# A post-norm layer of attention and a routed mixture of experts: last norm from accumulators, half-tile row buffers, two more ring slots, eleven more casts, other cast positions

## What is computed

```python
h = relu(einsum('td,ndf->ntf', flat, shared_w1) + b1)   # 2 shared experts, d_ff 1408
out = flat + einsum('ntf,nfd->td', h, shared_w2) + b2
scores = sigmoid(flat @ centroids.T) + bias              # 16 routed experts
gating = top-4 of scores, divided by their sum
out += sum_e relu(flat @ w1[e] + b1[e]) @ w2[e] * gating[e]
_layernorm(x) = (x - mean) / sqrt(var + 1e-5)
```

## Time and profile before

| what | value |
| --- | --- |
| time, median of 3 runs | 2623.97 us (2621.29 to 2628.06) |
| time of the profiled execution | 2625.21 us |
| its span, core 7 | 2623.6 us |
| spans of the other cores | 2576.4 to 2617.9 us |
| TensorE busy | 2201.3 us, 84% |
| VectorE, ScalarE, GpSimd busy | 855.9, 560.6, 378.0 us |

### The profile page before, as it was taken

How to read it: one execution, slowest core, us unless ns; L and a number is a source line. 1 busy time by engine, 2 the same in 40 slices (tenths; PEclk the granted TensorE clock), 3 DMA queues, 4 the chain that set the end, 5 groups by cost and what they waited for, 6 DMA issues and landing times.

```text
span 2623.6 us, 36177 instructions; the slowest of 8 cores (2576.4 to 2623.6 us)
## 1 busy us (share of the span) xinstructions
PE 2201.3 (84%) x13371; PEld 1205.6 (46%) x13371; DVE 855.9 (33%) x1390; ACT 560.6 (21%) x833; POOL 378.0 (14%) x583
## 2 busy tenths in 40 slices
PE   5879999989899669978977888899889897798576
PEld 3536646556465334433544545444545344344221
DVE  0234444444344334473311111113111131543454
ACT  0023433333343432301011111111111001011024
POOL 1001111010110000100021212122212202111100
PEclk9989999999999779999989988999999989898887
DMA  9599999999999799997489999989999979989963
GB/s 161 67 121 120 121 119 118 121 122 121 121 122 107 153 132 168 150 135 131 154 168 249 212 235 224 242 200 223 243 241 216 177 188 202 242 272 200 218 198 126
DMA packets 114970, 448.68 MB, mean 171 GB/s; under 512 B 16178, under 2 KB 16690, under 8 KB 105040
## 3 DMA queue, kind: packets, MB, share of 16 engines
q0 software_dynamic: 80208, 300.15, 74.8%
q1 hardware_dynamic: 34560, 145.70, 16.5%
HBM read 653.61 MB, written 145.23 MB: 304 GB/s over the span
## 4 chain that ended last, share of the span: by engine, by line
DMA 46%; PE 40%; DVE 5%; issue 4%; ACT 3%; POOL 1%; DVEq 0%; POOLq 0%; ACTq 0%; SPq 0%
DMA wpre<-w2x 11%; DMA wpre<-w1x 10%; PE PP L1210 9%; DMA ar<-w2x 8%; PE PP L1174 7%; DMA ar<-w1x 6%; DMA ar<-y_scr 5%; PE PP L815 4%; PE PP L639 3%; PE PP L793 3%; PE PP L341 3%; PE PP L360 2%; PE PP L1090 2%; ACT ar L496 1%; DMA ar<-xT 1%
## 5 line engine op out<-in xcount | busy, mean ns | idle before, releaser
L1174 PE MATMUL PP<-ar 128*128 128x256 bf16 (+1 forms) x2816 | 385.9, 296 | 81.2 <-DMA ar<-w1x 64.6
L1210 PE MATMUL PP<-ar 128*128 128x512 bf16 x1408 | 375.2, 405 | 21.0 <-DMA ar<-w2x 20.1
L1174 PEld LDWEIGHTS PP<-ar 128*128 128x128 bf16 x2816 | 279.8, 101 | 196.3 <-issue 110.3
L815 PE MATMUL PP<-ar 128*128 128x512 bf16 x704 | 214.5, 422 | 88.6 <-DVE ar L830 62.6
L341 PE MATMUL PP<-ar 128*128 128x512 bf16 x1024 | 245.8, 384 | 27.9 <-DMA ar<-wqkv 27.8
L496 ACT COPY ar<-PP 128x1024 bf16<-128x1024 bf16 (+1 forms) x192 | 153.4, 799 | 475.4 <-PE PP L485 475.4
L830 DVE SCALAR_TENSOR_TENSOR ar<-PP,ar 128x512 f32<-128x512 f32 x256 | 170.5, 688 | 229.3 <-PE PP L815 222.4
L360 PE MATMUL PP<-ar 128*128 128x256 bf16 x2048 | 241.5, 273 | 0.0
L1210 PEld LDWEIGHTS PP<-ar 128*128 128x128 bf16 x1408 | 132.3, 102 | 223.6 <-issue 106.6
L455 DVE TENSOR_REDUCE st_sb<-PP 128x1 f32<-128x256 f32 (+7 forms) x128 | 173.8, 1358 | 171.3 <-PE PP L449 162.3
L1099 DVE COPY ar<-PP 128x960 bf16<-128x960 bf16 x96 | 55.8, 599 | 503.8 <-PE PP L1090 503.7
(11 more groups left out here) (129 smaller groups left out, 1819.8 us busy)
## 6 DMA issues: line engine op xcount, KB each, us to landing
ar<-wpre SPq DMA_DIRECT2D x173, 512.0 KB, 8.2
ar<-w1x POOLq DMA_DIRECT2D x117, 512.0 KB, 15.3
ar<-w2x POOLq DMA_DIRECT2D x106, 512.0 KB, 20.5
wpre<-w2x POOLq DMA_DIRECT2D x92, 512.0 KB, 24.1
wpre<-w1x POOLq DMA_DIRECT2D x81, 512.0 KB, 24.7
ar<-y_scr SPq DMA_DIRECT2D x32, 1024.0 KB, 8.7
ar<-wqkv POOLq DMA_DIRECT2D x24, 1024.0 KB, 24.6
ar<-xT POOLq DMA_DIRECT2D x8, 1024.0 KB, 37.0
```

What stands on the lines that cost most here:

```text
L815: m = sb.mm((lambda e, j=j, w=w, bank=bank, ti=ti, dn=dn, last=last: e.matmul(psum_bank(bank), Hs[j][:, ti * 128:(ti + 1) * 128], w[:, dn ...
L1174: m = sb.either("tensor", j, *[[(lambda e, dc=dc, w=w, bank=bank, cols=cols: e.matmul(psum_bank(bank)[:, 0:cols], w[:, dc * 128:(dc + 1) * ...
L1210: m = sb.mm((lambda e, fc=fc, w=w, po=po, t=t, dn=dn, end=end: e.matmul(psum_bank(2 * t + dn), Hr(fc)[:, t * 128:(t + 1) * 128], w[:, po * ...
```

## The change

1. `precast` is issued at other places: no casts between the three weight loads of group 1, nine after them; 29 instead of 20 after the first feed-forward loads; and the rest (11) right behind `gather(0)`.
2. The list has 184 units: w1 of expert 12 is added ahead of its w2. `load_unit` now looks into `pre_mark`.
3. Two more slots (in the area of the former `y_in`) join the ring behind `gather(0)` and leave it at expert 12's start, where they become the first two of the half-tile buffers of the combine.
4. The combine loads half tiles (512 KB); a load is issued at every second step when a buffer is free, otherwise the oldest pending half is added and its buffer loaded anew. Ten half-tile buffers serve rank 3.
5. In the last group eight PSUM banks go round instead of three, L830 writes row sums by `accum_out`, squares are summed by ScalarE alone, and the scaling and the store of a tile follow one tile later. Ten half-tile adds are placed near the end of the first 128 matmuls; the other six follow one pair before each of the first three tile closings.

```diff
+PRE_FIRST = 9
+PRE_G0 = 29
-    units += [("w2", 2 + PRE_HALF, u) for u in range(FCH)]
+    units += [(kind, 2 + PRE_LAST, u) for kind in ("w1", "w2") for u in range(FCH)]
-                precast(PRE_ATTN)
+                precast(PRE_ATTN if g > 1 else 0)
         for kind in "qkv":
             next_w(kind, 1)
+        precast(PRE_FIRST)
...
+        def tail_squares(ti, parts):
+            ssq = tail_cols(ti)[1]
+            w = D // parts
+            for n in range(parts):
+                for dn in range(n * 4 // parts, (n + 1) * 4 // parts):
+                    sb.wait("scalar", *x_mark[ti, dn])
+                sb.wait("scalar", "ac")
+                sq_mark[ti] = sb.act(lambda e, n=n: e.activation(
+                    final_scr[:, n * w:(n + 1) * w], x_tm[ti][:, n * w:(n + 1) * w], AF.Square,
+                    accum_out=ssq[:, n:n + 1]))
+        def tail_scale(ti, parts):
+            s4, ssq, s1, var, rinv, bcol = tail_cols(ti)
+            sb.vchain(lambda e: e.reduce_sum(s1, s4, axis=AX.X))
+            sb.vchain(lambda e: e.scalar_tensor_tensor(var, s1, -1.0 / (D * D), s1, ALU.mult, ALU.mult))
+            sb.wait("vector", *sq_mark[ti])
+            for n in range(parts):
+                sb.vchain(lambda e, n=n: e.scalar_tensor_tensor(
+                    var, ssq[:, n:n + 1], 1.0 / D, var, ALU.mult, ALU.add))
+            sb.vchain(lambda e: e.tensor_scalar(var, var, EPS, None, ALU.add))
+            m = sb.vchain(lambda e: e.reciprocal(var, var))
+            sb.wait("scalar", *m)
+            m = sb.act(lambda e: e.activation(rinv, var, AF.Sqrt))
+            sb.wait("vector", *m)
+            return sb.vec(lambda e: e.scalar_tensor_tensor(bcol, s1, -1.0 / D, rinv, ALU.mult, ALU.mult))
...
-        precast(len(PRE_UNITS))
+        precast(PRE_G0)
         state["gen"] = dense_group(GROUPS[0], nt_outer=True)
...
         gather(0)
+        precast(len(PRE_UNITS))
+        ring["free"] += [(NSLOT, list_pe), (NSLOT + 1, list_pe)]
+        pump()
...
+        def combine_tick():
+            if not combine_load() and pend and todo:
+                combine_add()
+                combine_load()
...
+            if j == 12:
+                ring["leave"] = [NSLOT, NSLOT + 1]
+                ring["spare"] += [f for f in ring["free"] if f[0] >= NSLOT]
+                ring["free"] = [f for f in ring["free"] if f[0] < NSLOT]
+            if j >= 13:
+                todo.extend((j - 13, ti, hf) for ti in range(8) for hf in range(2))
...
-                if 13 <= j < 16:
-                    combine_step(j - 13, step)
+                if j >= 13 and step >= 2 and step % 2 == 0:
+                    combine_tick()
...
+            before = late.pop() if late else None
+            if before is not None:
+                ready = tail_scale(before, 1)
+            tail_squares(ti, 1 if ti < 7 else 2)
+            if before is not None:
+                tail_store(before, ready, False)
+            late.append(ti)
+            if ti == 7:
+                tail_store(7, tail_scale(late.pop(), 2), True)
...
+        for b in range(5):
+            give_bank(b, l2_free[b][0])
+        def close_tile(ti):
+            for _ in range(2):
+                if pend:
+                    combine_add()
+                    combine_load()
+            final_norm(ti)
+        for _ in dense_group(GROUPS[-1], bias2=True, after_tile=close_tile):
             count += 1
+            if count == 16:
+                while combine_load():
+                    pass
+            if count == 126:
+                for _ in range(10):
+                    combine_add()
+                    combine_load()
```

More of the change, by code:

```diff
@@ L48 @@
 PRE_EXPERTS = (0, 2, 4, 6, 8, 10, 14)
-PRE_HALF = 12
+PRE_LAST = 12
 def pre_units():
@@ new lines, in tail_store @@
+        def tail_store(ti, ready, last):
+            s4, ssq, s1, var, rinv, bcol = tail_cols(ti)
+            for hf in range(2):
+                xs = x_tm[ti][:, hf * 1024:(hf + 1) * 1024]
+                if last and hf == 1:
+                    sb.wait("vector", *ready)
+                    m = sb.vec(lambda e, xs=xs: e.tensor_scalar(xs, xs, rinv, bcol, ALU.mult, ALU.add))
+                else:
+                    sb.wait("scalar", *ready)
+                    m = sb.act(lambda e, xs=xs: e.activation(xs, xs, AF.Identity, bias=bcol, scale=rinv))
+                sb.wait("sync", *m)
+                sb.dma("sync", (lambda e, xs=xs, hf=hf: e.dma_start(
+                    out=out[ti * 128:(ti + 1) * 128, hf * 1024:(hf + 1) * 1024], in_=xs)), pool="store")
@@ L705, in emit @@
                 gate_scores(order[n - 1])
-        ring = {"free": [], "plan": [], "at": {}, "load": {}, "used": [], "spare": None}
+        ring = {"free": [], "plan": [], "at": {}, "load": {}, "used": [], "spare": None, "leave": []}
         for i in range(NSLOT):
@@ L744, in use @@
             if plans is None:
-                return ring_sb[0]
+                return slot_sb(0)
             sb.wait("tensor", *ring["load"][unit])
-            return ring_sb[ring["at"][unit]]
+            return slot_sb(ring["at"][unit])
         def release(unit, mark):
@@ L751, in release @@
                 return
-            ring["free"].append((ring["at"].pop(unit), mark))
+            slot = ring["at"].pop(unit)
+            ring["spare" if slot in ring["leave"] else "free"].append((slot, mark))
             pump()
@@ L778, in dense_group @@
         def dense_group(fcs, gate=None, bias2=False, after_tile=None, nt_outer=False):
+            ends = after_tile is not None
             h_ready = {}
@@ L1115, in emit @@
         y_freed = [[], []]
-        ybufs = [[y_in, None, None]]
         ring["spare"] = []
+        ybufs = []
         y_done = {}
-        def have_ybuf():
-            spare = dict(ring["spare"])
-            for s in sorted(spare):
-                if s in spare and s + 1 in spare:
-                    ybufs.append([carve(2048 * s, 4096, F32), spare.pop(s), spare.pop(s + 1)])
-            ring["spare"] = list(spare.items())
-            return len(ybufs) > 0
-        def combine_load(k, ti):
-            buf, m0, m1 = ybufs.pop(0)
-            for m in (m0, m1):
-                if m is not None:
-                    sb.wait("sync", *m)
+        pend = []
@@ L1133, in combine_load @@
+        todo = []
+        def combine_load():
+            ybufs.extend(ring["spare"])
+            ring["spare"] = []
+            if not (todo and ybufs):
+                return False
+            k, ti, hf = todo.pop(0)
+            slot, mark = ybufs.pop(0)
+            buf = slot_sb(slot).bitcast(F32)
+            sb.wait("sync", *mark)
             for i in range(13 + k):
                 sb.wait_all("sync", y_done[i])
-            for m in u_stored[-2:]:
-                sb.wait("sync", *m)
```

93 lines of the change are left out of this document (30 added, 63 removed).

## The result

| | before | after |
| --- | --- | --- |
| median of 5 runs | 2623.97 us | 2592.74 us |
| ratio, 95% interval | | 0.9857 (0.9828 to 0.9885) |
| profiled execution | 2625.21 us | 2580.38 us |
| its spans, mean of the 8 cores | 2601.8 us | 2566.6 us |

What follows compares the result with a forecast made beforehand. TensorE was taken as held back by casting DMAs in attention, DMA engines in the routed experts, VectorE in the combine and last group. From 2625.2 us, -32 + 22 - 12 - 22 - 23 = -67 gave median 2557 us, range 2514 to 2600.

Steps and rivals of the forecast that it cites:

- Early weight loads: Attention: group 1's weight loads no longer stand behind casts, so TensorE's later waits for them go; -32 us.
- 29 casts ahead of gather(0): Before expert 0: nine more casts delay gather(0), which lands 18 us later, plus 3 for the clock; +21 us.
- Eleven casts behind gather(0): Expert 0: gather(1) queues behind these casts and lands some 20 us later; +11 us (0 to +25).
- What follows from both: Gathers through later experts: +13 by the chain of waits, +34 at most by the DMA engines; taken as +22 us.
- Expert 12: Expert 12: w1 from `wpre` saves 21 us of DMA and TensorE's 10.5 us wait; -12 us (0 to -21).
- Half-tile combine: Combine, experts 13 to 15: VectorE hardly waits for loads, limited by 16 us of idle DMA time; -22 us.
- rival B: DMA engines bound the combine too, so its change and expert 12's bring nothing; 2591 us, chance 0.20 together with E.
- Last group: Last group: rank-3 adds end earlier, eight banks, norm a tile behind; 28 us less, 5 taken off for clock; -23 us.
- A: Experts and combine: the deeper ring pays in every pair and only VectorE's waits held the combine; 2518 us, chance 0.17.
- C: Last group stays bound by TensorE's lower clock, so the tail gains only 10 us; 2570 us, chance 0.09.
- D: From gather(0) on, late casts stay wholly on the path, 94 us, and DMA-bound gains are lost; 2663 us, chance 0.08.
- E: Attention: early loads do nothing because another wait takes their place; 2589 us alone, counted within rival B's 0.20.

Runs made afterwards that it cites:

- e1_early: Kernel before, with only attention's new cast positions (none between group 1's three loads, 29 instead of 20 casts ahead of gather(0)): 2631.48 us, ratio 0.9913.
- e6_drop9: Changed kernel with w1 and nine w2 units of expert 12 loaded directly, 20 casts ahead of gather(0), none behind: 2586.67 us, ratio 0.9742.
- e2_direct12: Changed kernel without the eleven casts of w1 of expert 12, so none behind gather(0): 2590.67 us, ratio 0.9752.
- e4_att9_g1: Changed kernel with nine casts moved from ahead of gather(0) to behind attention's last weight load, the last eleven behind gather(1): 2600.26 us, ratio 0.9761.
- e7_ring9: Changed kernel without the two added ring slots before expert 12: 2609.37 us, ratio 0.9912.
- e10_mix: Changed kernel with 164 casts: w1 of experts 12 and 14 and two w2 units of 14; 20 ahead of gather(0): 2568.88 us, ratio 0.9675.
- e12_noload: Changed kernel with the combine's loads of ranks 0 to 2 left out, their 48 half adds kept: 2520.75 us, ratio 0.9591.

## Why the prediction was half right

**Early weight loads: right in place and size** (-31.8 against -32). But its price belongs to it: the nine casts that leave attention are the nine that stand ahead of `gather(0)` now, and e1_early loses 29.6 us there. The prediction had their DMA work (9 x 4.4 = 40 us) and priced them at the new place only by a gather that is 18 us late.

**"29 casts ahead of gather(0)", +21: the step that failed first.** The mechanism was as described (the gather queues behind four casts in flight), the size was 29.9 + 4.7 = 34.6 (after against e6_drop9: 34.3). Three things add up. The prediction used 5.11 us per cast, read where casts run nearly alone. The last ones ahead of the gather go out every 6.3 us (1219.49 - 1213.18), beside ten `wpre` loads on the SP queue from 1177 on, so the gather goes out at 1228.15, not at the 1249.5 - 32 = 1217.5 expected. (That the last nine are casts of w1 is not the reason: in e2_direct12 they are of w2, and go out 6.1 to 6.8 us apart there.) And it lands 24 us after its issue, not 20. The clock behind the wait was allowed for with 3 us and took 4.7. The rule of the Trainium skill ("DMA: Bandwidth & Descriptors", Queues, rings and completion order), that an engine's descriptors of one queue start in ring order, agrees with the trace: 24 us behind four casts, against 6.8 in e6_drop9 on an idle queue (1214.55 to 1221.36). Of the two sums that the prediction set beside each other, +4 and +21, the larger one was too small. That the casts are the cause is shown (e6_drop9 has none of the 34 us). That the `wpre` loads are what slows the last of them is read from where they stand in time, and no run leaves them out.

**"Eleven casts behind gather(0)", +11: 18.4, and for another reason.** I had gather(1) late. It cost 2.4 us, and e4_att9_g1, which frees it, is no shorter. The casts fill the DMA engines from 0.6 to 0.9 of their time, and the `wpre` loads of expert 0, which come through another queue and so seemed out of reach, are late by 10.2 us; TensorE's busy time grows by 5.7.

**"What follows from both", the choice of +22: the error in kind.** I had two figures, +13 by the chain of waits and +34 by the DMA engines, and went between them. Measured is +48.1, above both. The relief of 19 us in experts 1 to 11 was to come from loads that start earlier in relation to TensorE and from two more slots. Together they gave 4.9, and by e7_ring9 the slots alone are worth at least that. At a DMA share of 0.97 there (1357 to 2173) loads did not run ahead. The idle time that I counted, 60 us, was taken as usable. Much of it lies where the gather must pass, and there it is used at the price of TensorE waiting (1215 to 1252: DMA share 0.98, TensorE busy 6.42 of 37 us).

**Expert 12, -12: too small.** It gave 18.0, and 22.8 against e2_direct12, about the whole 21 us of DMA time that its eleven units save. But what the eleven late casts cost in expert 0 (18.8) is returned here and little more, and the DMA share is 0.71 now. e10_mix, with w1 alone out of `wpre`, does the same with a share of 0.97: the casts of w2 of expert 12 are not needed.

**Half-tile combine, -22: half of it, by rival B.** TensorE's waits for VectorE fell by 19.8 us, near what was forecast, and TensorE's busy time by 2.9 with the clock. In return the waits for weights grew by 11.9. 19.8 + 2.9 - 11.9 = 10.8, and the stage is 10.1 shorter. The bound was in the prediction (16 us of idle DMA time) and was then passed with "some of expert 12's saving", which had not reached this stage. e12_noload shows it from the other side: what VectorE stands in front of is the load, and without these loads the waits for weights go as well. Finer buffers moved VectorE's waits off TensorE here; the bytes stayed.

**Last group, -23: right,** with errors that cancel. From the end of the first 128 matmuls to the last scaling the two profiled cores differ by (2616.3 - 2526.8) - (2568.5 - 2507.6) = 28.6 us; the prediction said 28, and took off 5 for a lower clock. The clock came back after three blocks of L849: the matmuls of these took 1.87 us for four, from 2531 on 1.04. Instead the span now ends 10.7 us after the last scaling (2579.2 - 2568.5), where before it was 7.3. The last store takes 4.9 us from its issue to landing (before 3.8) and lands at 2573.9; what is left, 5.3 us against 3.4, is the close of the program. ScalarE paces the tiles at 4.45 us, not 4.9.

**The rivals.** A (deeper ring pays everywhere) is out: e7_ring9. B was right for the combine and wrong for expert 12. C is out: the lower clock lasted 8 us on this core. D, that casts stay on the path, holds in its mechanism and not in its price: 20 casts cost 34.6 + 18.8 = 53.4 us, not 94, since the idle time did hide part. E has something of the truth: another wait does come, one stage later. The time lies at B's 2591, for a reason that is only half B's; that the result fell into the range is in part luck. Against the forecast the casts are 26 us worse and the combine 12, and expert 12 is 6 better.

What remains open: what the early loads are worth alone; whether w1 of expert 12 from `wpre` pays for its casts in all; and why the close behind the last store takes longer.

## What to carry to other kernels

When an edit moves DMA work out of one stage, book the same work at its new place with its full DMA time, and count idle DMA time there as usable only if nothing that the critical engine needs passes through it. A stage whose DMA share is near 1 gave back no more than its idle share here, whichever engine the waits are listed under. Preparing a weight in advance pays up to the unit at which its stage is bound by TensorE; where the DMA share then falls, as to 0.71 in expert 12 while TensorE is busy 74.10 of 76 us, more was prepared than that stage can use.
